# Graph hops by dense count strips: the table stationary and 512-column streams, in place of the strips stationary and 256-column streams

## The reference, cut to what matters

```
edge_index = stack([src, dst])                     # 212,500 edges, sorted by dst; 12,500 nodes, 128 features
h = maximum(layernorm(x), 0)
msg = where(type == 0, h[src] @ W_data.T + b_data, h[src] @ W_control.T + b_control)
x = x + relu(segment_sum(msg, dst) + h @ W_self.T + b_self)
h = maximum(layernorm(x), 0)
norm = rsqrt(deg)[src] * rsqrt(deg)[dst]
y = out = h
for _ in range(2):                                 # the two hops
    y = segment_sum(y[src] * norm, dst)
    out = out + y
x = x + out / 3
```

## Time and profile before

| | |
|---|---|
| median of 3 runs | 4000.37 us (3998.34 to 4006.49) |
| profiled execution, span | 3997.9 us |
| its own time beside the span | not recorded; the span is 2.5 us under the median of the runs |
| PE, PEld busy | 3405.9 us (85%), 2729.2 us (68%) |
| DVE, ACT, POOL busy | 2186.3 us (55%), 2329.7 us (58%), 2879.8 us (72%) |
| transfers | 571.77 MB, 143 GB/s over the span |

### The profile page before, as it was taken

How to read it: one execution, slowest core, us unless ns; L and a number is a source line. 1 busy time by engine, 2 the same in 40 slices (tenths; PEclk the granted TensorE clock), 3 DMA queues, 4 the chain that set the end, 5 groups by cost and what they waited for, 6 DMA issues and landing times.

```text
span 3997.9 us, 62254 instructions
## 1 busy us (share of the span) xinstructions
PE 3405.9 (85%) x23420; PEld 2729.2 (68%) x23420; DVE 2186.3 (55%) x3333; ACT 2329.7 (58%) x3075; POOL 2879.8 (72%) x3058
## 2 busy tenths in 40 slices
PE   7666777777777787777777899999998899999999
PEld 4344444444444444444444799999998899999999
DVE  7523888888888888888888422222222222222222
ACT  4001444444444444444444688888887788888887
POOL 2677777777777777777777577777776477777775
PEclk9788998999999999999999999999999999999999
DMA  6222333333333334333333566666666666666665
GB/s 194 85 61 61 109 119 121 113 109 110 126 109 110 114 110 128 110 109 125 110 115 112 170 179 187 192 192 187 189 189 184 179 179 176 187 182 181 179 184 145
DMA packets 367268, 571.77 MB, mean 143 GB/s; under 512 B 66678, under 2 KB 308225, under 8 KB 359283
## 3 DMA queue, kind: packets, MB, share of 16 engines
q1 hardware_dynamic: 270435, 370.74, 29.6%
q0 software_dynamic: 95664, 196.60, 19.2%
q10 hardware_dynamic: 864, 0.39, 0.0%
HBM read 424.48 MB, written 142.99 MB: 142 GB/s over the span
## 4 chain that ended last, share of the span: by engine, by line
PE 44%; POOL 38%; issue 13%; DVE 2%; DMA 2%; ACT 1%; SPq 0%; DVEq 0%; POOLq 0%; ACTq 0%
POOL rows L874 38%; PE wide L1175 34%; PE sums_bank L1091 7%; PE wide L1056 1%; ACT strip_ring L1011 1%; DMA stage<-hop_table 1%; DMA rows<-typed_table,index 0%; PE turned_bank L1126 0%; DVE big L1214 0%; DVE rows L1254 0%; DVE stage L1512 0%; POOL stage L914 0%; PE wide L1135 0%; DMA stage<-strips 0%; DMA big<-in_x 0%
## 5 line engine op out<-in xcount | busy, mean ns | idle before, releaser
L874 POOL DMA_INDIRECT rows<-typed_table,index x1661 | 1589.0, 957 | 506.0 <-issue 505.0
L874 POOL DMA_INDIRECT rows<-hop_table,index x1306 | 1251.9, 959 | 481.4 <-issue 394.9
L1011 ACT CAST strip_ring<-stage 128x1792 fp32r<-128x1792 uint8 x840 | 1409.2, 1687 | 285.3 <-PE wide L1175 279.2
L1175 PE MATMUL wide<-table_parts,strip_ring 128*128 128x256 f32 x11760 | 1461.0, 285 | 35.7 <-ACT strip_ring L1011 35.7
L1175 PEld LDWEIGHTS wide<-table_parts,strip_ring 128*128 128x128 f32 x11760 | 1431.3, 193 | 38.0 <-ACT strip_ring L1011 17.5
L1002 ACT CAST stage<-wide 128x392 uint8<-128x392 f32 x1920 | 790.3, 502 | 983.9 <-PE wide L1135 982.6
L1126 PE MATMUL turned_bank<-all_twos 128*128 128x512 bf16 x3328 | 1112.0, 394 | 0.0
L1091 PE MATMUL sums_bank<-rows,hot 128*128 128x129 f32 (+1 forms) x5934 | 801.2, 292 | 287.0 <-DMA rows<-typed_table,index 272.6
L1091 PEld LDWEIGHTS sums_bank<-rows,hot 128*128 128x128 f32 x5934 | 764.4, 206 | 337.8 <-issue 304.0
L1512 DVE TENSOR_TENSOR stage<-count_up,stage 128x1568 bf16<-128x1568 f32 x480 | 855.4, 1782 | 0.0
L1135 PE MATMUL wide<-stage 128*128 128x392 bf16 x1920 | 652.6, 340 | 221.8 <-DVE stage L1512 220.0
(11 more groups left out here) (141 smaller groups left out, 669.5 us busy)
## 6 DMA issues: line engine op xcount, KB each, us to landing
stage<-strips SPq DMA_DIRECT2D x840, 224.0 KB
strips<-stage SPq DMA_DIRECT2D x60, 1568.0 KB
rows<-typed_table,index POOLq DMA_INDIRECT x1661
rows<-hop_table,index POOLq DMA_INDIRECT x1306
resid<-xin SPq DMA_DIRECT2D x50, 256.0 KB, 3.0
hop_table<-scaled SPq DMA_DIRECT2D x50, 256.0 KB, 3.8
xin<-resid SPq DMA_DIRECT2D x50, 256.0 KB
typed_table<-rows SPq DMA_DIRECT2D x49, 256.0 KB, 2.1
```

The costliest lines, as they stand in the source:

```text
L874: pool.indirect_dma_start(out=rows[:, o % RING, c, 0:P], out_offset=None, in_=tables[k], in_offset=bass.IndirectOffsetOnAxis(ap=index[:, c ...
L1011: act.copy(strip_ring[:, number % STRIP_RING], counts_ring[place]).then_inc(strip_cast, 1)
L1175: last = pe.matmul(wide[:, nth % 4, 0:PARTS * P], strip_ring[:, number % STRIP_RING, b - first, :], table_parts[:, b, :, :].rearrange("p n ...
```

## The change

The roles in the dense matmul change places. One part of one table block is stationary, and a whole batch's strips, 4 tiles x 128 = 512 columns, stream against it, with both parts accumulated into the same 512 columns of PSUM. The sums then stand by features, so VectorE copies them to SBUF (`copy_sums`, a slot after the batch's last step) and TensorE turns them with 4 transposes (`turn_sums`, two slots after it, behind that slot's sum); `finish` reads the turned sums from PSUM. A step is now a batch by a piece of one batch (4 blocks, the last piece 2): 16 x 25 = 400 steps a hop, with 8 matmuls each. Its counts are 2048 contiguous bytes per partition, which each tile's store writes in pieces of 512 bytes, now with two transfers a tile. 16 batches are dense instead of 15, so the hops begin at group 135 and have 73 slots, 71 of them with dense steps (`SLOTS_LEFT = 2`). The count ring has 6 places instead of 7, the lead has 18 steps in both hops, the reload has 25 pieces of a batch, at most 5 in a slot, into 4 buffers, and the loads for the lead steps are issued over several slots.

```diff
-DENSE_BATCHES = 15
+DENSE_BATCHES = 16
...
-STEP_BLOCKS = 14
-COUNT_RING = 7
+COUNT_RING = 6
...
-RELOAD_BLOCKS = 7
-RELOAD_RING = 3
-RELOADS_AT_ONCE = 3
+RELOAD_RING = 4
+RELOADS_AT_ONCE = 5
...
     def order_of_steps(k):
...
+        late = last_of_pass[k - 1]
+        lead = [(0, piece) for piece in range(total) if piece not in late]
+        order = lead + [(0, piece) for piece in sorted(late)]
+        order += [(s, piece) for s in range(1, DENSE_BATCHES) for piece in range(total)]
+        return min(len(lead), LEAD_AT_ONCE * LAST), order
...
         def reload_start(piece):
-            return max([slot_stored(s) + 1 for s in reload_batches(piece)] + [slot_of_step(1, last_step_with(piece))])
+            return max(slot_stored(piece) + 1, slot_of_step(1, last_step_with(piece)))
...
                     sp.wait_ge(strip_kept, CELLS * (tile + 1))
-                    sp.dma_start(strips[tile], count_strips[tile % 2]).then_inc(strips_stored[tile % 2], 16)
+                    sp.dma_start(strips[s, :, 0:full * BATCH].rearrange("p (k t n) -> p k t n", k=total - 1, t=NODE_BLOCKS)[:, :, t, :],
+                                 made[:, 0:full, :].rearrange("p (k b) n -> p k (b n)", k=total - 1)).then_inc(strips_stored[tile % 2], 16)
+                    sp.dma_start(strips[s, :, full * BATCH:].rearrange("p (t n) -> p t n", t=NODE_BLOCKS)[:, t, :],
+                                 made[:, full:, :].rearrange("p b n -> p (b n)")).then_inc(strips_stored[tile % 2], 16)
...
-                            if leaving == event_at(k, events[k][-1][0]):
-
-                                load_counts_behind(number for at in range(slots_of(k), slots_of(k) + LAST) for number in steps_at(k, at))
+                        if i == events[k][-1][0] + 4:
+                            load_counts_behind(number for at in range(slots_of(k), i + 1) for number in steps_at(k, at))
+                        elif i > max(events[k][-1][0] + 4, slots_of(k) - 1):
+                            load_counts_behind(steps_at(k, i))
...
                     pe.wait_ge(strip_cast, number + 1)
-                    for b in range(first, end):
-                        last = pe.matmul(wide[:, nth % 4, 0:PARTS * P], strip_ring[:, number % STRIP_RING, b - first, :],
-                                         table_parts[:, b, :, :].rearrange("p n f -> p (n f)"),
-                                         start=(begins and b == first), stop=(ends and b == end - 1))
+                    moving = by_tile(strip_ring[:, number % STRIP_RING, :], piece)
+                    for b in blocks:
+                        for part in range(PARTS):
+                            last = pe.matmul(in_blocks(wide[:, nth % 2, :]), table_parts[:, b, part, :], moving[:, :, b - blocks[0], :],
+                                             start=(begins and b == blocks[0] and part == 0),
+                                             stop=(ends and b == blocks[-1] and part == PARTS - 1))
                     last.then_inc(strip_used, 1)
+
+                def turn_sums(k, s):
+                    nth = dense_number(k, s)
+                    pe.wait_ge(sums_copied, nth + 1)
...
+                    for b in range(NODE_BLOCKS):
+                        last = pe.transpose(wide[:, 2 + nth % 2, b * P:(b + 1) * P], own_in[:, nth % 2, b * P:(b + 1) * P], identity[:, :])
+                    last.then_inc(sums_turned, 1)
...
+                def copy_sums(k, s):
+                    nth = dense_number(k, s)
+                    if nth >= 2:
+                        dve.wait_ge(sums_turned, nth - 1)
+                    dve.wait_ge(strip_used, step_number(k, batch_steps(s)[1]) + 1)
+                    dve.tensor_copy(own_in[:, nth % 2, :], wide[:, nth % 2, :]).then_inc(sums_copied, 1)
```

More of the change, by code:

```diff
@@ L139, in gnn_kernel, with blocks_of_piece @@
     first_cut = [0, len(cuts[0]), len(cuts[0]) + len(cuts[1])]
[L144 to L148, removed]
+    steps_per_hop = DENSE_BATCHES * total
+    dense_slots = hop_groups - SLOTS_LEFT
+    def blocks_of_piece(piece):
+        return range(piece * NODE_BLOCKS, min((piece + 1) * NODE_BLOCKS, real_blocks))
     last_of_pass = [{total - 1}, {total - 1, DENSE_BATCHES - 1}]
     def order_of_steps(k):
[L153 to L159, removed]
+        late = last_of_pass[k - 1]
[3 more added lines that the diff above has]
+        return min(len(lead), LEAD_AT_ONCE * LAST), order
     lead_steps, orders = zip(*([(0, [])] + [order_of_steps(k) for k in range(1, HOPS + 1)]))
@@ L188, in hop_wanted @@
     def hop_wanted(k):
-        dense = [(tile_slot[k][(s + 1) * NODE_BLOCKS - 1], s) for s in range(DENSE_BATCHES)]
+        dense = [(batch_slot[k][s], s) for s in range(DENSE_BATCHES)]
         return dense + [(slot, s) for slot, s in cuts[k] if s >= DENSE_BATCHES]
@@ L534, in step_at, with batch_done_in, dense_number, piece_size @@
             return k + 1, j, *orders[k + 1][j]
-        def tiles_done_in(k, i):
-            return [t for t in range(DENSE_TILES) if tile_slot[k][t] == i]
+        def batch_done_in(k, i):
+            return batch_slot[k].index(i) if k and i in batch_slot[k] else None
+        def dense_number(k, s):
+            return (k - 1) * DENSE_BATCHES + s
+        def piece_size(piece):
+            return len(blocks_of_piece(piece)) * BATCH
+        def by_tile(ap, piece):
+            return ap[:, 0:piece_size(piece)].rearrange("p (t b n) -> p t b n", t=NODE_BLOCKS, n=P)
         TURN, PLACE, FETCH, CELLS_TURN, CELLS_AHEAD = 2, 4, 10, 2, 6
@@ L610, in reloads_of_slot, with reloads_before, turn_slot @@
             return [(r, piece) for r, (slot, piece) in enumerate(reload_order) if slot == i]
-        def reloads_before(first, end):
-            return max(r for r, (_, piece) in enumerate(reload_order)
-                       if piece * RELOAD_BLOCKS < end and (piece + 1) * RELOAD_BLOCKS > first) + 1
+        def reloads_before(piece):
+            return [p for _, p in reload_order].index(piece) + 1
+        TURN_AFTER = 2
+        def turn_slot(k, s):
+            return batch_slot[k][s] + TURN_AFTER
+        assert all(finish_slot(k, s) <= turn_slot(k, s + 2) for k in range(1, HOPS + 1) for s in range(DENSE_BATCHES - 2))
+        assert all(turn_slot(k, s) < hop_groups + LAST and finish_slot(k, s) > turn_slot(k, s) for k in range(1, HOPS + 1) for s in range(DENSE_BATCHES))
         assert all(lead_steps[k] <= LEAD_AT_ONCE * LAST for k in range(1, HOPS + 1))
@@ L1156, in dense_step @@
                 def dense_step(number):
-                    k, step, tile, piece = step_at(number)
-                    nth = (k - 1) * DENSE_TILES + tile
-                    first, end = piece * STEP_BLOCKS, (piece + 1) * STEP_BLOCKS
-                    begins, ends = step == tile_first[k][tile], step == tile_last[k][tile]
+                    k, step, s, piece = step_at(number)
+                    nth = dense_number(k, s)
+                    begins, ends = (step == edge for edge in batch_steps(s))
```

120 lines of the change are left out of this document (54 added, 66 removed).

## The result

The changed kernel takes 4008.8 us (10 runs, 4002.9 to 4011.4) against 4000.3 us before (10 runs): ratio 1.0019, 95% interval 1.001 to 1.0028. It is 0.2% slower, a small difference but one that the interval keeps clear of none; the forecast was 3944 us, and 3905 to 3995 doesn't hold the time. All medians in this document are over executions in the fast state; the one slow execution, 6701 us among four of the old form in bf16, is left out. The profiled execution took 4009.0 us, with a span of 4007.0.

What follows compares the result with a forecast made beforehand. TensorE was taken to bound both hops, GpSimd just behind; +6 (start of hop 1) - 23.7 (hop 1) + 8.6 (transition) - 46.7 (hop 2) = -56 us, from 4000.4 to 3944 us, range 3905 to 3995.

Steps and rivals of the forecast that it cites:

- What bounds the hops: Both hops: TensorE busy all the time, 10.17 us a slot, with GpSimd a bound only 0.2 us behind.
- The pace of the new matmul: Dense matmul of 512 columns: weight load hidden behind the longer stream, 0.2158 us each, 2992 a hop.
- The second half of rival 1: Dense matmul: only the fixed 13 ns stay, 0.2265 us a matmul, +64 us, 4008 us; chance 5%.
- The 16th batch: Both hops: 73 groups, not 82, so sums take 16.1 us less; its added matmuls lie within the 2992 x 0.2158 us.
- The casts: Strip casts on ScalarE: 1.89 us a step against TensorE's 1.73, covered during the sums, so nothing charged in steady running.
- Reloads in hop 1: End of hop 1: TensorE idle while table pieces reload, 30 us and 7 for the clock, 37 us.
- The 3 us for a fifth reload: Hop 1, five reloads sharing four buffers: the fifth waits for VectorE's part of the first, 3 us more.
- Transition: Between hops 1 and 2: reload 23 queued ahead of casts and batch 24's finish, 46 us, 8.6 more than today.
- Start of hop 1: Lead steps up to hop 1's first sum: +4 us for casts and +2 for the 512-byte stores, +6.
- nothing charged: Hop 0: 0.4 us more of VectorE in a slot's 10.0, absorbed by the ring of 4 gathered groups, no cost.
- Hop 2: Second hop: from 831.0 us to 784.3, 46.7 less.
- the 1.5 us kept for stalls: Hop 2: of today's 5.4 us of stalls 1.5 remain, the late reload now lying behind casts 12 to 14.

Runs made afterwards that it cites:

- the stream alone: A small kernel with nothing but streams of 32 matmuls each, the graph computation left out; plain f32 with 512 columns took 0.4300 us a record.
- The 128-column stream: Streams of 32 matmuls in a small kernel with the graph computation left out; f32r with 128 columns came 0.1102 us apart.

## Why the prediction was wrong

*What bounds the hops.* Right: TensorE, before and after, busy through both.

*The pace of the new matmul.* This is the step that failed. "I read this as the weight load setting today's warm pace at 0.12 us, and as hidden once the stream is longer. I take 0.2158 us." It is 0.2277, 11.9 ns more, and 35.6 us a hop. The 13 ns are paid by each f32r matmul, at 512 columns as at 256, and a longer stream doesn't hide them. The weight load is at most a part of them: at 256 columns half as many stationary columns save 6.4 ns, at 512 they save nothing. I had excluded a fixed cost by two observations that don't touch it. L1056 is plain f32 (4.7 ns over its two times 384 columns, and 3.3 over two times 512 in the stream alone), and I carried it over to f32r, which is another kind of matmul. And at the lower clock no excess shows, in the changed kernel either:

```profile
3063.88 1.65 PE L1184 MATMUL wide<-strip_ring,table_parts 128*128 128x512 f32 x3 [5.19 <-ACT strip_ring L1020]
...
3063.88 3.35 PE L1184 MATMUL wide<-strip_ring,table_parts 128*128 128x512 f32 x7 [5.19 <-ACT strip_ring L1020]
```

```profile
3064.00:3067.00 3.00, 3.00 (x7) 2.36 (x8) 0.65 (x1) 3.00 (x2) 2.29 (x3) 0.50 0.56 149
```

(3.35 - 1.65)/4 = 0.425 us where 512 columns at 1.2 GHz are 0.4267. But an excess that shows only at the higher clock is no sign of a hidden load. The bf16 matmuls behave alike: they are 2.5 ns over their columns at full clock, and in the changed kernel in bf16, behind a wait and at the lower clock, they show nothing either:

```profile
3025.71 4.02 PE L1184 MATMUL wide<-strip_ring,table_parts 128*128 128x512 bf16 x9 [4.94 <-ACT strip_ring L1020]
...
3025.71 5.73 PE L1184 MATMUL wide<-strip_ring,table_parts 128*128 128x512 bf16 x13 [4.94 <-ACT strip_ring L1020]
```

```profile
3026.30:3031.00 4.70, 4.70 (x13) 1.66 (x11) 0.18 (x1) 4.55 (x3) 3.48 (x5) 0.50 0.66 178
```

(5.73 - 4.02)/4 = 0.4275 us, against 0.4267. So the row could not separate the two readings. The second half of rival 1 (0.2265 us, 4008 us) had the mechanism, with a chance of 5%. That its time is met to a microsecond is partly luck: the pace was another 1.2 ns slower, 7 us in all, and the other terms of the sum made up for it by 6.

By the Trainium skill, page "TensorE: Matmul & The Clock Gate", section "LDWEIGHTS (loading the stationary operand)", the load takes 107 ns. The 128-column stream, 0.1102 us, is within 4 ns of that, though it does not show that the load is what paces it. The prediction took the row's 120 ns for a disagreement; it was none: 120 ns is what 256 columns take and 13 ns more, and the same 13 ns stand over 512 columns, a stream twice as long as the 107 ns.

*The 16th batch* was costed inside the sum, at the wrong pace, and never by itself. The sum had 196 x 0.2158 = 42 us against 16 us of sums a hop: a loss of 26 us a hop even so, in a forecast of 3944. That a part of the change made it slower stood in the numbers and was not said. The two runs with one part changed show it: -36 us for the swap with its new rings and orders (4000.3 to 3964.6), +44 for the batch.

*The casts*, priced at 1.89 us: 10.96 us for six, 1.83 each, against a step of 1.82. They stayed off the path.

*Reloads in hop 1*, 37 us: the mechanism was right, as the kernel without reloads shows, and the size was 28.4 (845.4 less 817.0): gaps of 4.1 to 5.4 us, and 9 for the lower clock and the casts' pace. The 3 us for a fifth reload did not appear: the gaps were forecast at 5.9, 9.0, 9.1 and 5.9 us and measured 5.2, 4.8, 5.4 and 4.1.

*Transition*, 46 us: 49.1, with a second gap of 5.22 us where the prediction's sequence of steps has nearly ten. Without reloads 36.1.

*Start of hop 1*, +6: +10.7. The last sum of hop 0 starts at 2238.97 instead of 2235.17, 3.8 us later, and "nothing charged" for hop 0 was off by about that. Whether the 32 more quads or the 512-byte stores do it stays open. From hop 0's first sum to the start of its last, the runs with 15 batches take 2092.0 and 2092.1 us with the old stores and 2093.2 and 2093.9 with the new; with 16 batches they take 2094.0 and 2094.5 with the old and 2094.1 to 2098.9 (five runs) with the new. Each may be worth a us or two, which is less than these five differ. The other 7 us lie behind hop 0, in the lead steps.

*Hop 2*: 2992 x 0.2277 + 129.9 + 16 x 0.36 = 817.0, measured 816.8. The transposes take 5.8 us of it, where the sum had 7.2. Of the 1.5 us kept for stalls nothing is left.

## What to carry to other kernels

A matmul's distance over its columns at full clock should be taken from a row of the same number format; if none exists at another width, two streams of 32 matmuls, of different widths, separate a cost that stays from one that hides behind a longer stream. A wider stream wins only what is paid for each matmul beyond its columns, here 13 ns for half as many matmuls, and never the 13 ns that the remaining ones still pay. And where a change bundles a new form with a new split of the work between engines, the split is costed by itself: taking work off the engine that isn't the bound, onto the one that is, costs its price (here 66 us in the old form and 44 in the new, where with 15 batches the relieved engine itself ended hop 2).

## What the runs showed of the hardware

At 2.4 GHz an f32r matmul costs 13 to 14 ns beyond its columns at 256, 384 and 512 columns (bf16 2.4 and 2.5 ns at 256 and 512; plain f32 3.3 ns over twice 512), whatever the bank or the accumulation; at 1.2 GHz nothing of it shows, nor of the 2.5 ns. With 64 stationary columns instead of 128 the excess halves at 256 streaming columns and does not fall at 512. Two bf16 parts instead of two f32r parts therefore took 73 us off a kernel of 4009 us. Four transposes of an f32 block of 128 columns take 0.36 us from their start to the next stream, and uint8 casts of 2048 columns run at 1.83 us each, one behind the other.
